# A second attention's preparation with its tables made earlier and its statistics taken at the first FFN's end, and both halves' FFN logits ahead of the routing

## The reference

```python
x = x + attn_a(ln(x))     # 16 heads of 8; softmax of minus a hyperbolic distance
x = x + ffn(ln(x))
x = x + attn_b(ln(x))     # 16 heads of 8; rotary q and k, biases, plain softmax
x = x + ffn(ln(x))        # the same weights as the first ffn

def attn_b(x):
    q, k, v = split(x @ qkv_w.T + qkv_b)
    q = q * cos + rotate_half(q) * sin
    k = k * cos + rotate_half(k) * sin
    return softmax(q @ k.T * 8 ** -0.5) @ v @ proj_w.T + proj_b

def ffn(x):
    scores = sigmoid(x @ router_w.T)             # 64 experts in 8 groups
    # of scores + e_bias: the 4 best groups (by the sum of their best two),
    # in them the 8 best experts; their scores, normalised, times 2.5
    coef = ...                                   # 2048 x 64, 8 of 64 not zero
    h = silu(x @ Wg) * (x @ Wu) * coef           # 64 experts of width 64, all computed
    return h @ Wd + (silu(x @ SWg) * (x @ SWu)) @ SWd
```

## Time and profile before

| | us |
|---|---|
| median of 3 runs (lowest, highest) | 1241.22 (1237.67, 1244.19) |
| the profiled execution | 1241.72 |
| its span in the profile | 1239.9 |
| TensorE busy | 996.3 (80%) |
| VectorE busy | 1023.0 (83%) |
| ScalarE busy | 733.1 (59%) |
| GpSimd busy | 324.3 (26%) |

### The profile page before, as it was taken

The page is one execution under the profiler, slowest core; times in us unless marked ns, Lnnn a source line. Parts: engine busy times, 40 slices in busy tenths (PEclk is TensorE's granted clock), DMA queues, the critical chain, the costliest instruction groups (busy, mean ns, idle before and its releaser), DMA issues. The chain is left out here.

```text
span 1239.9 us, 17589 instructions
## 1 busy us (share of the span) xinstructions
PE 996.3 (80%) x5292; PEld 707.9 (57%) x5292; DVE 1023.0 (83%) x1784; ACT 733.1 (59%) x886; POOL 324.3 (26%) x217
## 2 busy tenths in 40 slices
PE   4764667777742799999999687899725999999997
PEld 3543344444422577778777444555524877877876
DVE  5659888888727799999999777898276999999997
ACT  2437999999952455555555321677422555555554
POOL 2005555555530122233223121000000223222221
PEclk8765555555555899999999785899956999999999
DMA  1000000000000466666666000000002566666664
GB/s 51 1 1 1 1 1 1 1 1 1 1 7 9 108 149 152 136 154 152 144 146 154 31 0 1 1 2 1 1 7 62 136 148 157 148 141 158 152 141 96
DMA packets 26091, 85.25 MB, mean 69 GB/s; under 512 B 3904, under 2 KB 17088, under 8 KB 17856
## 3 DMA queue, kind: packets, MB, share of 16 engines
q1 hardware_dynamic: 26048, 84.70, 29.8%
HBM read 82.58 MB, written 2.10 MB: 68 GB/s over the span
## 5 line engine op out<-in xcount | busy, mean ns | idle before, releaser
L1112 ACT ACTIVATE sg<-ps 128x512 f32<-128x512 f32 x264 | 157.8, 598 | 126.9 <-PE ps L434 126.9
L1118 ACT ACTIVATE hh<-hf 128x512 fp32r<-128x512 f32 x264 | 167.1, 633 | 104.8 <-DVE hf L1744 104.4
L1738 DVE TENSOR_TENSOR hl<-hf,hh 128x512 fp32r<-128x512 f32 x264 | 186.3, 706 | 26.2 <-ACT hh L1118 6.7
L434 PE MATMUL ps<-xh,whi 128*128 128x512 f32 x528 | 206.9, 392 | 0.0
L434 PE MATMUL ps<-xl,whi 128*128 128x512 f32 x528 | 206.5, 391 | 0.0
L434 PE MATMUL ps<-xh,wlo 128*128 128x512 f32 x528 | 206.4, 391 | 0.0
L1744 DVE TENSOR_TENSOR hf<-h,cbc 128x512 f32<-128x512 f32 x256 | 194.8, 761 | 0.0
L1216 POOL TENSOR_TENSOR rr<-xr,rr 128x2048 f32<-128x2048 f32 x32 | 144.8, 4545 | 189.7 <-ACT xr L1003 185.6
L1731 DVE TENSOR_TENSOR h<-sg,ps 128x512 f32<-128x512 f32 x264 | 179.2, 679 | 16.5 <-PE ps L434 14.1
L1260 POOL CAST whi<-wraw 128x384 fp32r<-128x384 f32 x66 | 62.1, 940 | 478.7 <-PE ps L434 375.2
L434 PE MATMUL ps<-hh,whi 128*128 128x512 f32 x264 | 110.8, 420 | 7.6 <-DVE hl L1738 7.6
(11 more groups left out here) (246 smaller groups left out, 1594.3 us busy)
## 6 DMA issues: line engine op xcount, KB each, us to landing
cbc<-routing_coefficients SPq DMA_DIRECT2D x128, 512.0 KB, 6.0
wraw<-in_wexp_dram SPq DMA_DIRECT2D x66, 192.0 KB, 5.9
X<-in_x_dram SPq DMA_DIRECT2D x4, 256.0 KB, 4.5
routing_coefficients<-cT SPq DMA_DIRECT2D x8, 128.0 KB, 2.3
out_dram<-X SPq DMA_DIRECT2D x4, 256.0 KB, 2.8
cstb<-in_consts_dram SPq DMA_DIRECT2D x1, 648.0 KB, 3.5
wa<-in_wA_dram SPq DMA_DIRECT2D x1, 256.0 KB, 3.9
wb<-in_wB_dram SPq DMA_DIRECT2D x1, 192.0 KB, 3.7
```

The source lines that it names most:

```text
L434: return pe.matmul(o, l, r, start=start, stop=stop, **kw)
L1112: act.activation(sg[c % 2][:, :], bank(4 + 2 * (c % 2)), ACT.Silu).then_inc(s_sg, 1)
L1118: act.activation(hh[c][:, :], hf[c % 2][:, :], ACT.Copy).then_inc(s_hh, 1)
L1738: dve.tensor_tensor(hl[c][:, :], hf[c % 2][:, :], hh[c][:, :], ALU.subtract).then_inc(s_hl, 1)
```

## The change

1. `rope_tables` and the weight shuffles move from stage 5 to stage 3 of the first FFN (GpSimd's `rope_weights` behind its split of the shared expert's weights; TensorE's and ScalarE's part behind the logits of both halves; the signs on VectorE). SP's loads for them move too, in five pieces, ahead of the first coefficients, with a wait. The bias pair `b2` is copied by ScalarE instead of VectorE.
2. Stage 5's statistics are taken inside `experts(0)`'s end, each group right behind its residual sum; ScalarE's deviations follow its `yT` copies.
3. The scaling of the inputs goes from VectorE to ScalarE in stages 3, 5 and 7: one activation per tile with the reciprocal deviation as scale and an offset, minus mean by reciprocal, as bias. VectorE makes the offsets (`f_off`, `b_off`).
4. In stage 5 TensorE's order is split up: projections of g+1, q selections of g, values of g+1, transposes of g+2, k selections of g. Transposes go to bank 2.
5. `q`, `k` and `v` of the second attention have tensors of their own (`b_qt`, `b_kt`, `b_vt`), and the barrier between `prepare_b` and `samples_b` is gone; TensorE's first score tile waits for group 0's copies, its first shifted tile for all.
6. In stages 3 and 7 the statistics of all four groups come first, then the logits of both halves, then the first coefficients' transposes; the halves have banks, `f_xn`, `f_xT` and `sc` of their own. The last step of the second routing waits for the first coefficients' transposes, since `coef` is one tensor.

The diff, cut to its core (the SBUF plan, which is only regrouped so that the new tensors fit, and renamings are left out):

```diff
@@ sync
             load_shared(0)
+            sp.dma_start(rope_in[:, :], consts[:, C_COS:C_END]).then_inc(s_bin, 16)
+            sp.dma_start(w_in[:, :], wB[:, 0:2 * P]).then_inc(s_bin, 16)
+            sp.dma_start(bqk_s[:, :], bqk).then_inc(s_bin, 16)
+            sp.dma_start(wv_b[:, :], wB[:, 2 * P:3 * P]).then_inc(s_bin, 16)
+            sp.dma_start(bv_s[:, :], brow[0:1, 0:P].broadcast_to([P, P])).then_inc(s_bin, 16)
             sp.wait_ge(s_in, 16 * 4)
+            sp.wait_ge(s_bin, 16 * 5)
...
             meet(sp, 4)
-            sp.dma_start(cstb[:, :], consts).then_inc(s_bin, 16)
-            sp.dma_start(wb[:, :], wB[:, 0:3 * P]).then_inc(s_bin, 16)
-            sp.dma_start(bqk_s[:, :], bqk).then_inc(s_bin, 16)
-            sp.dma_start(bv_s[:, :], brow[0:1, 0:P].broadcast_to([P, P])).then_inc(s_bin, 16)
-            sp.wait_ge(s_bin, 16 * 4)
             meet(sp, 5)
-            meet(sp, 6)
@@ tensor: rope_tables, prepare_b
                 pe.wait_ge(s_perm, 1)
+                pe.wait_ge(s_xh, lap(0, 1, 0))
...
+            def xn_transposed_b(g):
+                pe.wait_ge(s_xn, GROUPS + g + 1)
+                if g >= 1:
+                    pe.wait_ge(s_u, 2 * g - 1)
+                for t in range(GTILES):
+                    last = pe.transpose(bank(2)[:, t * P:(t + 1) * P], b_xn[g % 2][:, t, :], ident)
+                last.then_inc(s_xnT, 1)
...
             def prepare_b():
-                rope_tables()
+                xn_transposed_b(0)
                 project_b(0)
-                pe.wait_ge(s_natc, 2)
+                values_b(0)
+                xn_transposed_b(1)
                 for g in range(GROUPS):
                     if g + 1 < GROUPS:
                         project_b(g + 1)
-                    select_b(g)
+                    select_q_b(g)
+                    if g + 1 < GROUPS:
+                        values_b(g + 1)
+                    if g + 2 < GROUPS:
+                        xn_transposed_b(g + 2)
+                    select_k_b(g)
...
+                if V == 0:
+                    pe.wait_ge(s_outL, 4 * GROUPS + 2)
+                    pe.wait_ge(s_outR, 3 * GROUPS + 2)
+                if U == 0:
+                    pe.wait_ge(s_outL, 6 * GROUPS)
+                    pe.wait_ge(s_outR, 5 * GROUPS)
@@ tensor: prepare_f
+            def spare(i, g):
+                return 4 * g + 2 * (1 - i)
...
                 logits(f, 0)
+                logits(f, 1)
+                if f == 0:
+                    rope_tables()
                 coefs_transposed(f, 0)
-                logits(f, 1)
                 coefs_transposed(f, 1)
@@ scalar
+            def norm_apply_b(g):
+                act.wait_ge(s_boff, g + 1)
+                if g >= 2:
+                    act.wait_ge(s_xnT, GROUPS + g - 1)
+                for j in range(GTILES):
+                    last = act.activation(b_xn[g % 2][:, j, :], X[:, g * GTILES + j, :], ACT.Identity,
+                                          bias=b_off[g][:, j:j + 1], scale=rstd[g][:, j:j + 1])
+                last.then_inc(s_xn, 1)
...
             def prepare_b():
+                norm_apply_b(0)
+                xT_b(0)
+                norm_apply_b(1)
+                xT_b(1)
                 for g in range(GROUPS):
-                    norm_std(1, g)
-                project_b(0)
-                rope_tables()
-                for g in range(GROUPS):
-                    if g + 1 < GROUPS:
-                        project_b(g + 1)
                     highs_b(g)
-                    select_b(g)
+                    if g + 2 < GROUPS:
+                        norm_apply_b(g + 2)
+                    select_q_b(g)
+                    if g + 2 < GROUPS:
+                        xT_b(g + 2)
+                    select_k_b(g)
...
             def prepare_f(f):
-                f_norm_std(f, 0)
+                f_norm_std(f)
+                f_norm_apply(f, 0)
                 f_norm_copy(f, 0)
-                f_norm_std(f, 1)
+                f_norm_apply(f, 1)
                 scores(f, 0)
-                coef_copies(f, 0)
                 f_norm_copy(f, 1)
                 scores(f, 1)
+                if f == 0:
+                    rope_tables()
+                coef_copies(f, 0)
                 coef_copies(f, 1)
@@ vector: prepare_b
                 for g in range(GROUPS):
-                    norm_stats(1, g, s_stat)
-                for g in range(GROUPS):
                     norm_scale(1, g)
...
-                norm_apply(0, b_xn[0], s_xn)
-                norm_apply(1, b_xn[1], s_xn)
...
+                for g in range(GROUPS):
+                    dve.scalar_tensor_tensor(b_off[g][:, :], mv[g][:, :, 0], -1.0, rstd[g][:, :],
+                                             ALU.mult, ALU.mult).then_inc(s_boff, 1)
...
                 for g in range(GROUPS):
-                    if g + 2 < GROUPS:
-                        dve.wait_ge(s_xnT, GROUPS + g + 1)
-                        norm_apply(g + 2, b_xn[g % 2], s_xn)
                     lows_b(g)
                     if g + 1 < GROUPS:
                         rope_parts(g + 1)
+                    select_q_b(g)
+                    if g + 1 < GROUPS:
                         v_biased(g + 1)
-                    select_b(g)
+                    select_k_b(g)
@@ vector: prepare_f, end of experts
-                f_norm(f, 0)
-                f_norm_apply(f, 0)
+                f_norm(f)
+                f_offsets(f)
+                if f == 0:
+                    rope_signs()
                 lows(f, 0)
-                f_norm(f, 1)
                 route(f, 0)
-                f_norm_apply(f, 1)
                 lows(f, 1)
                 route(f, 1)
...
+                if i == 1:
+                    dve.wait_ge(s_cT, lap(f, 0, 1))
...
+                    if f == 0:
+                        dve.wait_ge(s_res, c + 1)
+                        norm_stats(1, c, s_stat)
```

341 lines of the change are left out of this document (175 added, 166 removed).

## The result

Four executions of the changed kernel had a median of 1227.51 us (1226.69 to 1258.66) beside four of the kernel before at 1242.70 (1237.67 to 1247.04); the ratio is 0.9877, with a 95% interval of 0.9828 to 0.9926. The ratio leaves out the execution of 1258.66, the only slow one of the eight, at a mean granted clock of 0.766 where the others of its kernel had 0.804 to 0.807. The forecast was 1225.0, in a range of 1217 to 1234. The profiled execution took 1228.02 us, its span 1226.2.

A forecast was written before the change was run, and what follows sets the result against it. In three stretches, both routing preparations and the second attention's preparation, no engine is full and one chain decides. Terms -7.5 - 8.5 - 0.7 = -16.7 took 1241.7 to 1225.0 us, range 1217 to 1234.

The forecast's parts named there:

- Part 1: Routing preparation, both FFNs: gap between halves shrinks to 1.25 us, first routing starts 2.15 later; net -3.25 and -4.25.
- Part 2: Start of the second attention's preparation: VectorE's first rotation product at 710.0 instead of 712.65.
- Part 3: Second attention's groups: VectorE sets the pace at 7.6 us a group instead of 10.3; with Part 2, -8.5.
- The +3.0 for the clock: Second attention's groups: allowance for later projections at the low clock, half of 5.0, and 0.5 for late selections.
- rival 1: Clock holds: all later projections run at 2.4 GHz, 3.5 us more gained, 1221.5; chance 0.17.
- The +0.5 for GpSimd's addition: End of the second attention's preparation: cost of GpSimd's bias addition to X falling beside the last lows.
- -12.0: Second attention's preparation: first score maximum at 744.5, 12.0 us earlier, if everything holds at 2.4 GHz.
- Part 4: Exponential's table load goes ahead with the barrier gone: -0.7, of 1.28 the part TensorE waited; ends 0 and -1.3.
- The samples: Second attention's stage from first exponential to last addition to X: forecast to move by 0.
- Rival 4: Slower than before: samples stay at 1.2 GHz, 64 steps cost 0.76 each, 49 us, 1274; chance 0.03.
- Rivals 2, 3 and 5: 2: clock low in all groups, 1232, 0.12; 3: ScalarE activations 0.6 each, 1233, 0.05; 5: does nothing, 1239, 0.03.

The follow-up runs named there:

- before_again: The kernel before, unedited, run for a second profile; that profiled execution took 1262.03 us.
- logits_back: Changed kernel, but TensorE transposes the first half's coefficients ahead of the second half's logits in the routing preparations; median 1242.8 us.
- apply_late: Changed kernel, but ScalarE makes the first half's sigmoids ahead of its applications for the second half; median 1252.8 us.
- bias_late: Changed kernel, but GpSimd's bias addition to X waits until VectorE's last low parts are made; median 1244.6 us.
- fill: Changed kernel plus twelve extra 128x512 full-row products in the score steps ahead of the first shifted scores; median 1248.7 us.
- both_24: Changed kernel with the edits of bias_late and apply_late, plus a full-row 128-column product in sample steps 0 to 23 only; median 1218.91 us.
- fill_steps: Changed kernel with fill's twelve products, plus a full-row 256-column product in each of the 64 sample steps; median 1243.3 us.
- both_fill: Changed kernel with the edits of bias_late, apply_late and fill, plus a full-row 128-column product in each of 64 steps; median 1233.1 us.

## Why the prediction was right, and where it wasn't

**Part 1** was right in size and cause: -3.15 and -4.27 against -3.25 and -4.25 (against before_again the first is -4.15 as well; its gap was 7.63). The price of an application, put together from rows of other forms at 0.37, measured 0.387 (eight in 3.19), and logits_back shows the gap to be TensorE's order. What it overlooked is that the order of ScalarE left 2.4 us more per FFN (apply_late).

**Part 2** forecast the way in the new order to 0.1: the profile after starts this stage 4.26 us earlier, so the first rotation product was forecast at 705.74 and came at 705.78. But the 2.6 us that it counts as won are gone when the comparison is with before_again, where TensorE's clock rose before group 0's projection and the old order took 15.58.

**Part 3** named the right engine and pace (7.1 to 7.4, forecast 7.6) and mis-sized two terms. The +3.0 for the clock was 0: here rival 1 had it right and the forecast did not, for the clock was 1.00 from 706 to 730, and as long in each profile of a changed kernel. The +0.5 for GpSimd's addition was +1.9 (bias_late). So -12.0 + 1.9 is near the -10.56 of parts 2 and 3 together, where the forecast had -8.5. (Rival 1 prices the clock at 3.5; the terms of the sum give 3.0, for the +0.5 is not the clock's.) Against before_again the two parts are -6.7, so a forecast between the two readings owes something to the execution that was profiled.

**Part 4**, -0.7, was 1.35: all of the load, as the upper bound had it, not the part that TensorE was seen to wait. On the switch's price by the Trainium skill, "ScalarE: Activation LUTs", What ACT_TABLE_LOAD costs, the trace stays against the 1.38 us of drain: the load at 375.39 ends at 376.67, and the sigmoid starts at 376.68 behind it, and eight applications end at 375.37, 0.02 ahead of it.

**The samples** were the step that failed: they stood in the sum at nothing, and cost 6.7. That the total is 3 us from the forecast all the same is luck, 2.6 more won in the priced parts than forecast and 6.7 lost here; the same kernel's next profile took 1233.98, with 65 us at the low level in this stage instead of 33. Rival 4 had the mechanism (samples that stay at 1.2 GHz) with 3 in 100, and its own sign, a clock of 0.5 beyond the sixth step, came. Its price for a stage all at the low level, 49 us, was too high: apply_late's took 156.2, 37 more than the 119.2 of the line. What was wrong is that it was a rival of the change at all: the row on which it rested, a clock at 1.00 some six steps in, was one execution of a kernel whose 78 have low-clock times from 453 to 595. **Rivals 2, 3 and 5** did not occur: no later group ran at 0.50, no application took 0.6, and the gaps are gone.

So the change is worth 13 us at equal low-clock time (-13.2, error 0.7). By stages it is more, 19.3 against the profile before and 16.5 against before_again, since the stages that it shortens run mostly at the low level and it takes 15 to 20 us of that along, worth 4 to 5. The clock in the samples may add or hide as much as the whole change in a single execution. Open stays whether the change makes long stretches more frequent: eight of the 56 executions of changed kernels without extra products had low-clock times of 577 to 592, against one of 78 before with 595; on the chip that six of the eight come from, it was six of 22 against none of 13. It also stays open which property of the extra products counts, and why the clock of fill fell back from 1.00 behind its products where both_24's held; no run varied that alone.

## What to carry to other kernels

Before a stage is costed at nothing, ask at which clock it ran in the profiled execution and whether other executions ran it at the same: with two levels, the mean granted clock and the span of each run give the low-clock time, and a line through them tells an edit of 2 us from a clock that moves 30, if each kernel has some ten executions. Profile the kernel before twice as well: here its second profile took 4 us off the gain of one part. Where a long stage sits at the low level with TensorE busy, a few extra products at its start, into a bank that is about to be overwritten, can be cheaper than what the level costs, as 24 were here and 64 were not; try the smallest dose first. And when a barrier goes, look at what it kept apart: here it kept a GpSimd addition away from VectorE's two-input subtractions.

## What was not expected of the hardware

TensorE stayed at 1.2 GHz for 84 us in which it was busy in all of them (fill, 773 to 857), mostly in products on 32 rows and value products with 32 columns of weights; and with products over the full rows between them it was at 2.4 GHz 9 to 10 us after the first of these in three profiles (fill, fill_steps, both_fill) and 15 us in both_24's. The Trainium skill, "TensorE: Matmul & The Clock Gate", Part 1, says that activity releases the throttle; if activity is read as the busy time of the profile, these 84 us stand against it.

One VectorE instruction of 0.69 us took 3.36 beside a GpSimd addition of 4.51 that had started 1.70 earlier, and ended 0.55 behind it, while one with its input in PSUM was not touched.
